# Attention values and sums in TensorE's column groups, the angle offset joined to the rounding, and a rewritten merge table

## What is computed

```python
# layer 0, attention: q, k, v of 16 heads of 8 values
q = (query @ Wq + bq).reshape(B, Nq, 16, 8); k = ...; v = ...
attn = softmax(einsum('bhqd,bhkd->bhqk', q, k) * 8 ** -0.5)   # 77 keys
out = einsum('bhqk,bhkd->bhqd', attn, v).transpose(...) @ Wo + bo
...
# layer 1, filter of the state-space part (s4d), for 128 channels x 64 states
dtA = dt[:, None] * (A_re + 1j * A_im)
powers = exp(dtA[:, :, None] * arange(L))
K = 2.0 * einsum('dn,dnl->dl', dC, powers).real
```

## Time and profile before

| | us |
|---|---|
| median of 3 runs (551.55 to 557.5) | 553.52 |
| the profiled execution | 553.78 |
| its span | 552.0 |
| PE matmul busy | 478.6 (87%) |
| DVE busy | 430.9 (78%) |
| ACT busy | 264.7 (48%) |
| POOL busy | 117.0 (21%) |
| L865, 80 instructions | 43.1 |

### The profile page before, as it was taken

One profiled execution on the slowest core, in us unless ns is written; L12 is line 12 of the kernel. 1 busy time (PEld: TensorE's weight loads), 2 busy tenths in 40 slices (PEclk: granted clock), 3 DMA queues, 4 the chain that ended last, 5 costly groups with the idle time before them and its releaser, 6 DMA issues.

```text
span 552.0 us, 8986 instructions
## 1 busy us (share of the span) xinstructions
PE 478.6 (87%) x2883; PEld 370.6 (67%) x2883; DVE 430.9 (78%) x1781; ACT 264.7 (48%) x549; POOL 117.0 (21%) x198
## 2 busy tenths in 40 slices
PE   4386586799999999999999999999999999736971
PEld 3154234598975989848987985689878989514760
DVE  4378988885625787886797988899898789998667
ACT  4441466575456465564538456534474544411040
POOL 4522003122020031003015210310222331232021
PEclk9998595699999999999999999999999999956996
DMA  7900770002100004000003000000000000000000
GB/s 182 173 2 0 222 220 0 2 1 39 21 2 2 1 1 58 4 1 1 2 0 51 9 4 1 2 20 0 2 2 1 2 20 1 1 1 0 21 0 19
DMA packets 16176, 15.03 MB, mean 27 GB/s; under 512 B 1210, under 2 KB 14274, under 8 KB 16130
## 3 DMA queue, kind: packets, MB, share of 16 engines
q1 hardware_dynamic: 16130, 14.47, 11.7%
HBM read 9.15 MB, written 1.05 MB: 18 GB/s over the span
## 4 chain that ended last, share of the span: by engine, by line
PE 70%; DVE 22%; ACT 3%; issue 3%; POOL 2%; DMA 1%; DVEq 0%; POOLq 0%; ACTq 0%
PE moe_h L910 20%; PE moe_y L922 20%; PE side L865 5%; PE side L970 3%; PE side L980 2%; PE side L958 2%; DVE area L1394 2%; PE moe_h L932 2%; PE side L1001 2%; PE side L772 2%; DVE TOP L1384 1%; PE side L944 1%; PE side L989 1%; PE side L834 1%; PE side L1023 1%
## 5 line engine op out<-in xcount | busy, mean ns | idle before, releaser
L1132 ACT ACTIVATE HT<-moe_h,W 128x256 f32<-128x256 f32 x256 | 115.5, 473 | 104.0 <-PE moe_h L910 103.8
L910 PE MATMUL moe_h<-xnT_moe,W 128*128 128x256 f32 x512 | 138.0, 387 | 0.8 <-ACT HT L1132 0.7
L922 PEld LDWEIGHTS moe_y<-W,HT 128*128 128x128 f32 x1024 | 131.3, 192 | 8.8 <-issue 3.2
L922 PE MATMUL moe_y<-W,HT 128*128 128x128 f32 x1024 | 134.9, 276 | 0.0
L910 PEld LDWEIGHTS moe_h<-xnT_moe,W 128*128 128x128 f32 x512 | 88.3, 193 | 17.8 <-issue 7.2
L1370 DVE SCALAR_TENSOR_TENSOR X<-moe_y,RW,X 128x128 f32<-128x128 f32 x128 | 38.9, 346 | 8.1 <-PE moe_y L922 7.1
L865 PE MATMUL side<-PT,VP 128*72 128x512 f32 x80 | 43.1, 625 | 1.2 <-ACT PT L1112 1.2
L1394 DVE MATCH_REPLACE8 area<-TOP,area 128x77 f32<-128x77 f32 x192 | 40.9, 230 | 0.0
L932 PE MATMUL moe_h<-W 128*128 128x256 f32 x112 | 31.7, 436 | 0.0
L1384 DVE MAX8 TOP<-area 128x8 f32<-128x77 f32 x192 | 31.5, 230 | 0.0
L1704 POOL TENSOR_TENSOR area<-area 128x128 f32<-128x128 f32 x16 | 7.4, 463 | 110.3 <-ACT area L1155 110.3
(11 more groups left out here) (323 smaller groups left out, 851.8 us busy)
## 6 DMA issues: line engine op xcount, KB each, us to landing
W<-in_w SPq DMA_DIRECT2D x8, 512.0 KB, 7.7
QA<-Q SPq DMA_DIRECT2D x24, 128.0 KB, 4.4
X<-in_x SPq DMA_DIRECT2D x4, 256.0 KB, 6.5
KM<-area SPq DMA_DIRECT2D x6, 160.0 KB, 5.9
out_dram<-FO SPq DMA_DIRECT2D x3, 256.0 KB, 2.3
V<-in_vpack SPq DMA_DIRECT2D x1, 579.0 KB, 7.7
area<-in_r2pack SPq DMA_DIRECT2D x1, 576.0 KB, 8.0
area<-in_gpack SPq DMA_DIRECT2D x1, 576.0 KB, 8.5
```

The lines of the kernel that those rows point to most:

```text
L910: pe.matmul(moe_h[n % 2][:, 0:HS], W1[:, e, c * P:(c + 1) * P], xnT_moe[:, b % 2, h * HS:(h + 1) * HS], start=True, stop=True).then_inc(mo ...
L922: mm = pe.matmul(moe_y[m % 2][:, t * P:(t + 1) * P], HT[:, m % 2, c, t * P:(t + 1) * P], W2[:, e, c, :], start=(c == 0), stop=(c == HC - 1))
L1132: act.activation(HT[:, m % 2, c, :], moe_h[n % 2][:, 0:HS], ACT.Relu, bias=wc("b1")[:, e * HC + c:e * HC + c + 1]).then_inc(moe_h_ready, 1)
```

## The change

1. **Column groups.** Values and sums go to two banks. A group's five exponential tiles are kept (PT has five buffers in place of two), and the products are made in four rounds a batch: for each of the two groups of pairs one round over its four full tiles and one over its left-over tile. In a round the four tiles go to the four 32-column groups of PE, first with ZP (or ZL) for the sums, then with VP (or VR) for the values; the sums come out already spread over the rows of their head. The spreading matmuls (L872) and ACT's copies go; DVE takes the reciprocal of one bank and multiplies with the other. The rows of Wo and of the value bias are permuted to match. VP is filled once for all batches on POOL (sixteen small products), VR by eight small ACT copies during set-up.
2. **Angle offset.** The offset and the rounding constant are added by one instruction; a three-operand instruction subtracts the constant and the angle, and the sine on ACT is taken with a negative scale and an offset operand. The angle step has five DVE instructions in place of seven, the rotation three in place of four.
3. **Merge table.** ORDER is written anew for all streams.

```diff
-NPT = 2
+NPT = NG
+ROUNDS = 4
...
-    for h in range(SC + 1):
-        if h < SC:
-            out.append(("score", b, h))
-        if h >= 1:
-            out.append(("pv", b, h - 1))
-        if h == NG + 1:
-            out.append(("attn_sum", b, 0))
+    for g in range(2):
+        for n in range(NG):
+            out.append(("score", b, g * NG + n))
+            if g == 1 and n == 0:
+                out.append(("pv", b, 1))
+        out.append(("pv", b, 2 * g))
+    out += [("pv", b, 3), ("attn_sum", b, 0), ("attn_sum", b, 1), ("o_proj", b, 0), ...
...
-S H2 S H5 K H2 K W2 F2 W2 F W2 F W6 F H3 K H K2 H2 W K H2 K H18 K8 H W K H2 K H2 K3 H E10 H E6 H2 K E2 K H C2 K E6 K
+H2 S2 H5 W K2 H F W10 F3 W F H3 K2 W2 H K3 H5 K2 H K2 H8 K H K5 H2 K H4 E3 K2 E3 K E2 K H E H E K E3 H2 E H K C E9 H
...
-                    mm = pe.matmul(dst[0:GROWS, :], VP[:, g, n, :], PT[:, i % NPT, :], start=(n == 0), stop=(n == NG - 1))
+                    for n, vr in enumerate((ZL, VR)):
+                        dst = side[FILL[("pv", b, 0, n)][0]]
+                        for q in range(NM):
+                            c = slice(32 * q, 32 * q + 32)
+                            if rest:
+                                mm = pe.matmul(dst[c, :], vr[c, b, g, :] if n else vr[c, g, :], PT[c, NM, :], start=False, stop=(g == 1), tile_position=(32 * q, 32 * q))
+                            else:
+                                mm = pe.matmul(dst[c, :], VP[:, b, g, q, :] if n else ZP[:, g, :], PT[:, q, :], start=(g == 0), stop=False,
+                                               tile_position=(0, 32 * q))
...
-                if kind == "attn_norm":
-
-                    dst, full = free_for(pe, kind, b, i)
-                    for g in range(2):
-                        pe.wait_ge(rz_ready, 2 * b + g + 1)
-                        mm = pe.matmul(dst[64 * g:64 * g + 64, :], cc("spread")[64:GROWS, :], ZR[g][64:GROWS, :],
-                                       start=True, stop=True)
...
-                    act.activation(VS[:, 1].rearrange("p b d -> p (b d)"), src[:], ACT.Copy).then_inc(read, 1)
+                    act.wait_ge(va_ready, 4)
+                    for q in range(NM):
+                        c = slice(32 * q, 32 * q + 32)
+                        for g in range(2):
+                            ins = act.activation(VR[c, :, g, 16 * g + HD0:16 * g + 16],
+                                                 src[c, :].rearrange("p (b d) -> p b d", b=B)[:, :, 64 * g + 16 * q + HD0:64 * g + 16 * q + 16],
+                                                 ACT.Copy)
...
-                if kind == "attn_sum":
-                    src, read = filled(act, "pv", b, 0, i)
-                    if b >= 1:
-                        emptied(act, "attn_norm", b - 1, 0)
-                    act.activation(ZR[i][64:GROWS, :], src[64:GROWS, :], ACT.Copy).then_inc(rz_ready, 1)
-                    act.activation(OV[64 * i:64 * i + 64, :], src[0:64, :], ACT.Copy).then_inc(read, 1)
...
-                    act.activation(G1b[:], G1b[:], ACT.Sin, scale=TWO_PI).then_inc(g_act, 1)
+                    act.activation(G1b[:], G1b[:], ACT.Sin, scale=-TWO_PI, bias=cc("cosrad")).then_inc(g_act, 1)
...
+                if kind == "attn_sum":
+                    src, read = filled(dve, "pv", b, 0, i)
+                    if i == 0:
+                        dve.reciprocal(OT[:], src[:]).then_inc(read, 1)
+                    else:
+                        emptied(dve, "pv", b, 0, 0)
+                        dve.tensor_tensor(OT[:], OT[:], src[:], ALU.mult).then_inc(read, 1)
...
-                    gelem(("x1", i), dve.tensor_scalar(G1b[:], G1a[:], cc("cosoff"), None, ALU.add))
-                    gelem(("x2", i), dve.tensor_scalar(G2a[:, :, 0:CA], G1b[:], ROUND, ROUND, ALU.add, ALU.subtract))
-                    gelem(("x", i), dve.tensor_tensor(G1b[:], G1b[:], G2a[:, :, 0:CA], ALU.subtract))
...
+                    dve.tensor_scalar(G1b[:], G1a[:], cc("cosoff"), ROUND, ALU.add, ALU.add).then_inc(g_dve, 1)
+                    gelem(("y1", i), dve.tensor_scalar(G1c[:], G1a[:], cc("sinoff"), ROUND, ALU.add, ALU.add))
+                    dve.scalar_tensor_tensor(G1b[:], G1b[:], ROUND, G1a[:], ALU.subtract, ALU.subtract).then_inc(g_dve, 1)
...
-                    gelem(("e3", i), dve.tensor_scalar(G2a[:], G2b[:], ROUND, ROUND, ALU.add, ALU.subtract))
-                    gelem(("e2", i), dve.tensor_tensor(G2b[:], G2b[:], G2a[:], ALU.subtract))
+                    gelem(("e0", i), dve.tensor_tensor(G2a[:], r1, cv, ALU.mult))
+                    gelem(("e1", i), dve.tensor_scalar(G2b[:], G2a[:], cc("cosoff"), ROUND, ALU.add, ALU.add))
+                    gelem(("e2", i), dve.scalar_tensor_tensor(G2b[:], G2b[:], ROUND, G2a[:], ALU.subtract, ALU.subtract))
```

More of the change, by code:

```diff
@@ L247, in needed @@
     if kind == "v_place":
-        return [("pv", b - 1, SC - 1)] if b >= 1 else [("setup_v", 0, 0)]
+        return [("setup_v", 0, 0)]
     if kind == "x_bo":
-        return [("v_place", b, 0), ("ln_apply", b, "attn")]
+        return [former, ("ln_apply", b, "attn")]
     if kind == "attn_sum":
-        return [("pv", b, NG * (i + 1) - 1)]
+        return [("pv", b, ROUNDS - 1)] if i == 0 else [former]
     if kind == "smax_T":
@@ L255, in needed @@
     if kind == "score":
[L256 removed]
+        return [("smax_T", b, 0)] + ([("pv", b, round_of(i - NPT))] if i >= NPT else [])
     if kind == "pv":
[L258 removed]
+        return [("score", b, NG * (i // 2) + (NM - 1 if i % 2 == 0 else NM)), ("v_place", 0, 0)] + ([former] if i >= 1 else [])
     if kind == "norm_T" and i == "moe" and b >= 2:
@@ L300, in needed @@
     if kind == "kgen_ang" and i == 0:
-        return [former, ("setup_rhs", 0, 0), ("setup_film", 0, B - 1)]
+        return [former, ("setup_rhs", 0, 0), ("setup_film", 0, B - 1), ("v_place", 0, 0)]
     if kind == "kgen_mul":
@@ L385, in place_fills @@
             take((kind, b, i, n))
-        if kind == "pv" and i % NG == 0:
-            held.add(take(("pv", b, 0, i // NG)))
+        if kind == "pv" and i == 0:
+            for g in range(2):
+                held.add(take(("pv", b, 0, g)))
         if kind == "attn_sum":
@@ L602, in recurrent_layers @@
         K3 = view("first", [P, 3, B, KW], BF16)
+        VS = view("first", [P, B, D])
         bvb = view("first", [P, P])
@@ L867, in _ @@
-                if kind == "attn_norm":
-                    dst, full = free_for(pe, kind, b, i)
-                    for g in range(2):
-                        pe.wait_ge(rz_ready, 2 * b + g + 1)
-                        mm = pe.matmul(dst[64 * g:64 * g + 64, :], cc("spread")[64:GROWS, :], ZR[g][64:GROWS, :],
-                                       start=True, stop=True)
-                    mm.then_inc(full, 1)
+                    g, rest = i // 2, i % 2
+                    if i == 0:
+                        for n in range(2):
+                            free_for(pe, "pv", b, 0, n)
+                        if b == 0:
+                            pe.wait_ge(v_placed, 1)
+                            emptied(pe, "setup_v", 0, 0, 4)
@@ new lines, in _ @@
+                    for n in range(NM, NG) if rest else range(NM):
+                        emptied(pe, "score", b, NG * g + n)
+                    for n, vr in enumerate((ZL, VR)):
[7 more added lines that the diff above has]
+                                               tile_position=(0, 32 * q))
+                        if i == ROUNDS - 1:
+                            mm.then_inc(side_full[FILL[("pv", b, 0, n)][0]], 1)
```

144 lines of the change are left out of this document (62 added, 82 removed).

## The result

Before 554.01 us (median of 20 runs), after 551.2 us (median of 20), ratio 0.9952, 95% interval 0.9929 to 0.9975: 2.8 us or half a per cent less, where 8 us were forecast. The time lies in the range, the direction is right, the size is not. The profiled execution took 549.6 us with a span of 547.8 (before 553.78 and 552.0).

A forecast was written before the change was run, and what follows sets the result against it. DVE bounds the front and end, PE the middle. Terms -5.7 + 0.3 - 5.5 + 4.5 - 1.0 = -7.4 us on the profiled 553.8 us gave 546 us, range 538 to 557.

The forecast's parts named there:

- What bounds each stage: Whole kernel: DVE's queue up to the first expert, PE in the middle, DVE after the last expert.
- Column groups, -5.5 us: Attention values and sums: 7.9 us a batch for 9.7, saving 5.5 us over batches 1 to 3.
- (c): Column groups: f32 groups go in program order, 2.15 us a set instead of 0.86; 587 us, chance 0.05.
- (d): Column groups: the groups share less than fully, 1.2 to 1.4 us a set; 557 to 563 us, chance 0.08.
- Angle offset and the front, -5.7 + 0.3 us: Up to the first expert: 5.7 us gained by shorter DVE work and new order, 0.3 lost to VR copies.
- The router's 0.8 us: Front: the router now stands behind the first experts, counted as 0.8 us gained.
- Middle, with the new table, +4.5 us: Expert stretch: new PE waits on DVE in batches 2 and 3 lose 4.5 us (0 to 10).
- two named places: Middle: PE waits for DVE's attention product, 2.3 us in batch 2 and 2.2 in batch 3.
- End, -1.0 us: From batch 2's last forward DFT on: DVE-bound with the same work, 1 us gained (3 gained to 3 lost).
- Rival (b): DVE keeps the time: PE's saving returns as waits in batches 2 and 3; 552 us (548 to 557), chance 0.26.

The follow-up runs named there:

- k_only: The kernel before with the angle offset joined to the rounding and nothing else; ratio to before 0.9945.
- after_local: The kernel after with one or two expert steps drawn in front of six steps for which PE waited; ratio to before 0.9899.
- new_nokgen: The kernel after with the old angle code, all else new; ratio to before 1.0009.
- after_oproj: The kernel after with two expert steps drawn in front of batch 2's output projection only; ratio to before 0.9921.
- best1: The kernel after with the old table, the reciprocal at its old place, and expert steps drawn forward at three places where PE waited; ratio to before 0.9894.
- after_oldtail: The kernel after with the steps behind its last expert matmul in the order of the table before; ratio to before 1.0057.
- k_tail: k_only with the steps behind the last expert matmul in the order of the kernel after; ratio to before 0.9952.
- best2: best1 with the steps behind the last expert matmul in the order of the kernel after; 546.23 us, ratio to before 0.9863.
- cg_oldtab: The kernel after with the table of the kernel before, each round standing where the product of its last tile stood; ratio to before 1.0234.

## Why the prediction was wrong

- **What bounds each stage**: right. k_only shows DVE's length in the front, after_local shows that PE's waits count in the middle.
- **Column groups, -5.5 us**: right and a little low, -6.9 us. A set takes 0.88 us, 0.97 where a change of shape follows, the round 1.88 (1.97 assumed). Rivals (c), f32 groups in program order at 2.15 us a set, and (d), 1.2 to 1.4 us, are refuted by the same rows. The Trainium skill (TensorE: Matmul & The Clock Gate, "What overlaps and what doesn't") says that matmuls start and end in program order. That section gives no time for a set; the 2.15 us are what the prediction made of that rule. The trace does not bear that reading out: eight f32 matmuls of four groups take 0.88 us, what two of one full-width call took.
- **Angle offset and the front, -5.7 + 0.3 us**: up to the first expert the times came to within 0.6 us, the reciprocal's partly by luck (DVE and not PE released it). Taken to the end of the third unit the front gives 3.1 us, 2.3 less than forecast. The router's 0.8 us was counted as a gain although it only moves behind the first expert matmul, and what its steps cost there was left out: DVE waits 2.23 us for its exponential, and PE 1.43 us for DVE. In the medians, the angle offset is 3.0 to 3.2 us (k_only, new_nokgen). The offset operand on ACT, taken as nothing, costs 0.09 us a sine (0.63 to 0.72 us for 128x512, 1.04 to 1.13 for 128x1024), 1.1 us of ACT in all.
- **Middle, with the new table, +4.5 us**: this is the step that failed. It priced two named places and nothing else. The one in batch 2 came (1.58 us for 2.3), the one in batch 3 did not come (2.2 taken); but some 7 us more lie in about twenty waits and holds of 0.2 to 0.9 us, at a text query, FiLM, a feed-forward product, a transposed norm, and in expert matmuls. 9.1 us in place of 4.5, more than the column groups save. That these are steps set down one or two expert steps too early is shown in part: after_local moved six such places, and its middle is 1.9 us shorter of the 4.2 us they held (2.9 us in the medians, where the intervals touch); after_oproj, with the one place that the forecast had named, got 0.4. best1 shows the column groups in an order with fewer waits: 345.6 us where the order before took 346.8. Of the 6.9 us saved in columns that is still only 1.2.
- **End, -1.0 us**: -3.9 us in the profiled execution, at a granted clock of 0.88 for 0.82, which the forecast did not price. after_oldtail is 5.8 us slower in the medians, k_tail no faster; what the order by itself is worth there stays open.
- **Rival (b)**, 548 to 557, had the time and half of the mechanism: PE's saved columns given back as waits. But it is not DVE's length that takes them (after_local's middle is shorter with the same DVE work), though the largest single wait is for DVE's product, and they are not in two projections.

The last expert matmul stood forecast at 457 to 461 us; it came at 467.0, 0.9 us ahead of before. best2 has it at 460.3. The forecast's terms as measured in the profiled execution: front -3.1, column groups -6.9, waits of the middle +9.1, tail -3.9 and the rest of the span +0.6: -4.2 us, and -2.8 in the medians. Two misses that gave less (front 2.3, middle 4.6) and two that gave more (column groups 1.4, tail 2.9) partly cancel; that the time lies within the range owes something to that.

## What to carry to other kernels

Where one list sets the order on all engines, a shorter step on one engine gives its time only if the list is made to fit it: count the places at which another engine's result was just in time before, not only those next to the edited step. When a code change and a new order come together, time each with the other's partner first; here it showed that the smallest edit carried the whole gain. Then read the list of waits, draw one or two steps of independent work in front of the largest, keep the steps that free its buffers ahead of it, give back behind it what was drawn, and read from the trace how much of the wait turned up behind: here more than half.

## What the runs showed of the chip

**A wait of the same length at the same place can cost more than twice as much.** after and after_oldtail have the same order up to here, and PE waits 1.43 us for the router's weights in both. In after the clock stayed at its upper level and the eight matmuls of L911 took 1.12 us [the rows above]; in after_oldtail:

```profile
112.11 0.60 PE L905 MATMUL side<-C,RW 128*8 128x128 f32 x4 [1.43 <-DVE RW L1368]
...
113.43 1.91 PE L912 MATMUL side<-B,xT_head 8*128 8x128 f32 x8 [0.29 <-issue]
115.27 1.22 PE L923 MATMUL moe_h<-xnT_moe,W 128*128 128x256 f32 x2
116.29 1.91 PE L935 MATMUL moe_y<-W,HT 128*128 128x128 f32 x8
```

with windows of a mean clock of 0.72 and 0.83, and the third unit ends at 122.6 in place of 118.0, though it was only 1.3 us behind at the wait:

```profile
110.00:118.00 8.00, 6.28 (x32) 5.27 (x31) 4.34 (x14) 3.85 (x8) 1.91 (x1) 0.72 0.00 0
118.00:125.00 7.00, 7.00 (x42) 6.43 (x42) 5.79 (x12) 2.76 (x6) 1.01 (x1) 0.83 0.00 0
```

In the same way the 1.64 us at 343.76 in cg_oldtab were followed by 3.4 us for two sets instead of 1.8. A short wait in a full stretch thus has two prices, its own length and that of a stretch at the lower of the two clock levels (1.2 for 2.4 GHz) behind it, and between after and after_oldtail the order of the instructions did not decide which was paid. It may be part of why the runs of after_oldtail lie as far apart as 554.74 and 561.42 us; that is not shown.

**VectorE beside POOL.** In the kernel after, the rounding pair of the rotation takes 0.75 and 1.23 us where POOL is idle, as forecast, and about twice that in the set that falls on POOL's exponent products. Timelines of DVE and of POOL:

```profile
62.71 0.75 DVE L1601 TENSOR_SCALAR area<-area,C 128x1024 f32<-128x1024 f32 x1
63.50 1.23 DVE L1602 SCALAR_TENSOR_TENSOR area<-area 128x1024 f32<-128x1024 f32 x1
...
73.15 1.43 DVE L1601 TENSOR_SCALAR area<-area,C 128x1024 f32<-128x1024 f32 x1
74.61 2.82 DVE L1602 SCALAR_TENSOR_TENSOR area<-area 128x1024 f32<-128x1024 f32 x1
```

```profile
72.71 1.32 POOL L1761 TENSOR_TENSOR area<-area,C 128x512 f32<-128x512 f32 x1 [24.10 <-PE side L1035]
74.11 2.24 POOL L1762 TENSOR_TENSOR area<-area,C 128x1024 f32<-128x1024 f32 x1
```

The new table moved the norm's four rows out of such a stretch (3.70 to 1.12 us) and this pair into one, which the forecast had not seen; it is one of the two reasons why DVE came late to the reciprocal.
